# Inner weights of product 4: their stores placed between GpSimd's loads of product 1's inner weights, their rounding spread

## The reference, cut to what matters

```python
q_emb = relu(cond @ W3 + b3)
v = (n * x + sum_over_tokens(x)) * q_emb           # n = 512 tokens
y = relu(v @ W2 + b2)                              # stage 1: 1024 x 1024 weight
base = y @ W_base + b_base                         # stage 2: 1024 x 1024 weight
shared = (y @ A_s) @ B_s
gates = top 2 of softmax(y @ W_router + b_router)
routed = sum over 6 experts of (gate * (y @ A_r[e])) @ B_r[e]
out = x + base + shared + routed
```

## Time and profile before

| what | value |
|---|---|
| median of 3 runs | 1413.12 us (1412.42 to 1414.57) |
| the profiled execution, its own time | 1414.27 us |
| its span, first to last instruction | 1412.4 us |
| mean granted TensorE clock over the span | 0.992 of full speed |
| TensorE busy | 1388.9 us, 98% of the span |
| VectorE, ScalarE, GpSimd busy | 1037.6, 664.0, 79.5 us |
| moved by DMA | 255.63 MB, mean 181 GB/s |

### The profile page before, as it was taken

The page is one execution under the profiler, slowest core; times in us unless marked ns, Lnnn a source line. Parts: engine busy times, 40 slices in busy tenths (PEclk is TensorE's granted clock), DMA queues, the critical chain, the costliest instruction groups (busy, mean ns, idle before and its releaser), DMA issues. The chain is left out here.

```text
span 1412.4 us, 18365 instructions
## 1 busy us (share of the span) xinstructions
PE 1388.9 (98%) x6069; PEld 1139.6 (81%) x6069; DVE 1037.6 (73%) x1700; ACT 664.0 (47%) x1209; POOL 79.5 (6%) x170
## 2 busy tenths in 40 slices
PE   9999999999999999999999998699999999999999
PEld 6888888888888888888888886488888888888887
DVE  6976777675776768678879575777777877778665
ACT  7774756556465664746544232333333432244221
POOL 3000100000000000000000001100000000000000
PEclk9999999999999999999999999799999999999999
DMA  8244836445273542528728379638566485756734
GB/s 314 84 156 119 258 123 179 154 126 156 67 204 117 156 140 76 171 96 274 255 73 262 120 235 320 209 107 266 196 233 239 143 274 183 267 181 188 242 119 160
DMA packets 151327, 255.63 MB, mean 181 GB/s; under 512 B 40416, under 2 KB 40672, under 8 KB 151232
## 3 DMA queue, kind: packets, MB, share of 16 engines
q1 hardware_dynamic: 135680, 199.75, 43.5%
q0 software_dynamic: 14688, 53.48, 12.1%
q10 hardware_dynamic: 864, 1.22, 0.2%
HBM read 171.69 MB, written 82.71 MB: 180 GB/s over the span
## 5 line engine op out<-in xcount | busy, mean ns | idle before, releaser
L2760 PE MATMUL ps<-act_hi,w_hi 128*128 128x512 f32 x1504 | 586.5, 390 | 8.5 <-DVE act_lo L1749 8.5
L2761 PE MATMUL ps<-act_lo,w_hi 128*128 128x512 f32 x1504 | 585.6, 389 | 0.0
L2762 PE MATMUL ps<-act_hi,w_lo 128*128 128x512 f32 x1504 | 585.6, 389 | 0.0
L2760 PEld LDWEIGHTS ps<-act_hi,w_hi 128*128 128x128 f32 x1504 | 282.7, 188 | 69.4 <-DVE act_lo L1749 10.1
L2762 PEld LDWEIGHTS ps<-act_hi,w_lo 128*128 128x128 f32 x1504 | 282.7, 188 | 58.7
L2761 PEld LDWEIGHTS ps<-act_lo,w_hi 128*128 128x128 f32 x1504 | 282.8, 188 | 58.5
L1010 ACT ACTIVATE act_hi<-src 128x512 fp32r<-128x512 f32 x208 | 125.0, 622 | 92.2 <-PE ps L2762 91.6
L1749 DVE TENSOR_TENSOR act_lo<-src,act_hi 128x512 fp32r<-128x512 f32 x192 | 129.5, 685 | 21.2 <-ACT act_hi L1010 21.1
L1029 ACT ACTIVATE yhi<-buf 128x512 fp32r<-128x512 f32 x128 | 80.2, 626 | 81.8 <-PE ps L2762 81.4
L1817 DVE SCALAR_TENSOR_TENSOR buf<-ps,bb_sb,buf 128x512 f32<-128x512 f32 x91 | 67.4, 748 | 64.7 <-PE ps L2762 61.0
L2760 PE MATMUL ps<-act_hi,inner_w 128*128 128x512 f32 x252 | 100.4, 398 | 10.7 <-issue 8.7
(11 more groups left out here) (181 smaller groups left out, 1656.6 us busy)
## 6 DMA issues: line engine op xcount, KB each, us to landing
src<-in_xT SPq DMA_DIRECT2D x224, 256.0 KB, 3.6
y_scratch<-buf SPq DMA_DIRECT2D x128, 256.0 KB, 3.0
src<-y_scratch SPq DMA_DIRECT2D x128, 256.0 KB, 5.2
inner_w<-inner_scratch POOLq DMA_DIRECT2D x63, 512.0 KB, 3.8
outT<-buf SPq DMA_DIRECT2D x115, 256.0 KB, 4.5
inner_scratch<-staged POOLq DMA_DIRECT2D x21, 512.0 KB, 4.9
wl_raw<-in_wbase SPq DMA_DIRECT2D x7, 1024.0 KB, 5.7
partner<-y_scratch POOLq DMA_DIRECT2D x12, 512.0 KB, 5.9
```

Of the source, the lines that this page charges most:

```text
L2760: nc.tensor.matmul(out, wh, a_h, start=start, stop=False, skip_group_check=onto)
L2761: nc.tensor.matmul(out, wh, a_l, start=False, stop=False, skip_group_check=onto)
L2762: return nc.tensor.matmul(out, wl, a_h, start=False, stop=stop, skip_group_check=onto)
```

## The change

Blocks 14 and 15 are rounded behind all four `high(9, 6, j)` and no longer wait for a store; blocks 16 and 17 behind all four `high(10, 0, j)`; block 18 moves from the end of pair 9 into `even`, and 19 and 20 move back by one place each, 20 into the middle of the four roundings of product 2. GpSimd stores 14 and 15 right behind `begin`, 16 and 17 behind `partner`, and 18, 19 and 20 each behind one load of `stream`. `partner4` is loaded between m = 5 and m = 6, in all three of the runs that have one. The two halves of the last store count on one semaphore.

```diff
+        FIRST_OF_TWO = tuple((e_of, 1) for e_of, n_of in RUNS if n_of == 4)
...
-            sp.wait_ge(last_half_stored, 16)
             for j in range(H):
                 sp.wait_ge(buf1_stored[j], 16 * 2 * ALL)
-                sp.wait_ge(buf2_stored[j], 16 * ALL)
+                sp.wait_ge(buf2_stored[j], 16 * (ALL + (j == H - 1)))
...
             def stream(r):
                 for m in range(2, L2):
                     inner_weights(r, m)
+                    if r == EARLY and m < 5:
+                        store_weights(2 * L2 + 2 + m)
+                    if m == 5 and RUNS[r] in FIRST_OF_TWO:
+                        load_partner4(RUNS[r][0])
...
             for e in range(EARLY, len(QUADS)):
                 begin(RUN[e, 1])
+                if e == EARLY:
+                    store_weights(2 * L2)
+                    store_weights(2 * L2 + 1)
                 load_partner(e)
                 if e == EARLY:
-                    for c in range(2 * L2, 3 * L2):
-                        store_weights(c)
-                load_partner4(e)
+                    store_weights(2 * L2 + 2)
+                    store_weights(2 * L2 + 3)
                 stream(RUN[e, 1])
...
                 if k >= 3:
                     act.wait_ge(inner_w_sum, sums_no(c // L2, k - 2))
-                if c >= 2:
+                if c >= 2 and k >= 2 or c // L2 == 1:
                     act.wait_ge(inner_w_stored[c % 2], 16 * (c // 2))
...
                 inner_high(r, 1)
                 if e == EARLY:
-                    inner_weight_high(3 * L2 - 2)
+                    inner_weight_high(2 * L2 + 4)
                 copy_p0(g, 0)
                 lr_high_a(p)
                 inner_high(r, 2)
+                if e == EARLY:
+                    inner_weight_high(2 * L2 + 5)
                 copy_p0(g, 1)
                 copy_p0(g, 2)
-                if e == EARLY:
-                    inner_weight_high(3 * L2 - 1)
                 for j in range(H):
                     high(g, 2, j)
+                    if e == EARLY and j == 2:
+                        inner_weight_high(2 * L2 + 6)
...
                     if g == SECOND - 1 and j in (0, 1):
                         inner_weight_high(L2 + 5 + j)
-                    elif g == SECOND - 1:
-                        inner_weight_high(2 * L2 + j - 2)
+                if g == SECOND - 1:
+                    inner_weight_high(2 * L2)
+                    inner_weight_high(2 * L2 + 1)
                 for j in range(H):
                     high(g + 1, 0, j)
-                    if g == SECOND - 1 and j > 0:
-                        inner_weight_high(2 * L2 + 1 + j)
+                if g == SECOND - 1:
+                    inner_weight_high(2 * L2 + 2)
+                    inner_weight_high(2 * L2 + 3)
...
                 inner_t2(r)
                 if e == EARLY:
-                    inner_weight_low(3 * L2 - 2)
+                    inner_weight_low(2 * L2 + 4)
                 lr_low_a(p)
                 add_p0(r, 0)
                 inner_low(r, 2)
                 inner_t3(r)
+                if e == EARLY:
+                    inner_weight_low(2 * L2 + 5)
                 add_p0(r, 1)
                 for j in range(H):
                     t2(g, j)
-                if e == EARLY:
-                    inner_weight_low(3 * L2 - 1)
                 for j in range(H):
                     low(g, 2, j)
+                    if e == EARLY and j == 2:
+                        inner_weight_low(2 * L2 + 6)
...
                     if g == SECOND - 1 and j == 1:
                         inner_weight_low(2 * L2 + 2)
                         inner_weight_sums(2)
-                    elif g == SECOND - 1 and j > 1:
-                        inner_weight_low(2 * L2 + 1 + j)
+                    elif g == SECOND - 1 and j == 2:
+                        inner_weight_low(2 * L2 + 3)
```

More of the change, by code:

```diff
@@ L272, in adaln_ffn @@
         x21_added = sem("x21_added")
-        last_half_stored = sem("last_half_stored")
         inner_hi_done = sem("inner_hi_done")
@@ L1685, in _ @@
             act.wait_ge(c21_done, four(ALL - 1, H - 1) + 1)
-            act.dma_start(outT[2 * LAST, K - 1, :, T // 2:T], buf2[:, H - 1, T // 2:T]).then_inc(last_half_stored, 16)
+            act.dma_start(outT[2 * LAST, K - 1, :, T // 2:T], buf2[:, H - 1, T // 2:T]).then_inc(buf2_stored[H - 1], 16)
         @block.vector
```

## The result

The changed kernel takes 1397.33 us (median of 4 runs, 1396.03 to 1397.85) against 1413.84 us (4 runs) for the kernel before, measured beside it: ratio 0.9883, interval 0.9865 to 0.9900, that is 16.5 us or 1.2% less. The forecast was 1395.2 us in a range of 1391 to 1402. The profiled execution took 1397.85 us, its span is 1396.0 us, 16.4 us shorter than before, at a mean granted clock of 0.996.

The account below looks back on a forecast made before the run. TensorE, busy 98% of the span, was taken as the bound, so only its stops and slow clock could be won: 4.4 + 2.2 + 8.8 + 2.5 = 17.9 us less, from the median 1413.12 to 1395.2 us, range 1391 to 1402.

Parts of the forecast that it names:

- the clock: TensorE's stop before `low(10, 0, 2)`, shortened to 4.2 us, keeps full clock; inner product 0 takes 2.72 us: 2.2 us less.
- Rival B: The clock falls in what is left of the first stop; the 2.2 us are not won: 1397.5 us; chance 0.27.
- The place of stores 14 and 15: Ahead of `partner` on GpSimd's queue, store 14 lands at 876.2 after 7.0 us; TensorE restarts at 881.1.
- Block 18: Moved from ahead of `inner_low(r, 0)` on VectorE, it lets the first inner product follow the restart 0.6 us sooner.
- The removed wait: Blocks 14 and 15 without waiting for a store: TensorE's 0.46 us wait at 864.45 goes, adding nothing to the sum.
- the place of `partner4`: Loaded between m = 5 and m = 6 in three runs; no margin for m = 6's load, but costed at nothing.
- The second stop: TensorE's wait before inner product 2 in pair 10 goes: 8.8 us, plus 2.5 us for its slow matmuls.
- the first 4.4 us: Passage from pair 9 to 10: the first inner product starts at 886.6 instead of 891.05, 4.4 us earlier.
- Rival E: GpSimd's list becomes a chain, loads m = 3 to 5 late behind stores 18 to 20: slower, 1423 us; chance 0.04.

Follow-up runs that it names:

- The filled kernels: Useless matmuls added to the changed kernel in the gaps before k = 2, k = 3 and inner product 0 (12, 6, 8): 1397.24 us, once more 1396.34 us.
- the repetition: The changed kernel run once more, unaltered, beside the kernel before: 1397.50 us, ratio 0.9896.
- the first of the two later versions: Against the changed kernel, blocks 16 to 20 all rounded in pair 10, `partner` ahead of store 14, stores two, one, two behind loads m = 2 to 4: 1392.26 us.

## Why the prediction was right, and where its sum was not

**The sign, the size and the range** came as forecast, and so did both places in the timeline. Of the sum of 17.9 us, 16.4 came.

**The step that failed** is *the clock*: "I take it that the clock holds, just." That rested on two falls, 4.3 and 4.4 us after the last matmul, taken as a fixed delay, against a stop of 4.2. The delay was not fixed: in the first profile of the changed kernel the fall came 2.5 us after the last matmul, within a stop of 3.7. In the two later profiles of that kernel it came after 4.7 us, with the stop already over. So the comparison failed on both sides: a stop shorter than the delay did not keep the clock, and the three matmuls at its end did not save it. Inner product 0 took 4.47 us, and the term of 2.2 us gave 0.45. Rival B came, with the 1397.5 us that it was given, and its chance of 0.27 was too low. The Trainium skill, "TensorE: Matmul & The Clock Gate", section "Why this matters for your kernels", had spoken for B: idleness between bursts brings the lower clock. By it the sum was about 15.7; the trace agrees, with 16.2 by its terms. The filled kernels show the price in the trace, 1.6 to 2.5 us.

**The place of stores 14 and 15** was right in kind and mis-sized in a term: the landing took 8.7 us (8.3 in the repetition, 869.24 to 877.51) where I took 7.0, between bounds of 2.9 and 9.3. In the first profile it did not show, by luck, since `begin` happened to be 1.7 us early; in the repetition, with `begin` at 868.19, TensorE restarted at 882.37, 1.3 us later than summed. The 4.86 us from ScalarE's start to TensorE's restart held in both. With `partner` ahead of the stores the restart comes about 2 us later.

**Block 18** was right: 0.6 us, 0.8 in the medians. **The removed wait and the place of `partner4`** were right to be priced at nothing; each put back moves nothing that can be measured.

**The second stop** was right to the row: no wait is left there, and with the old order of the queue it is back. What I had not seen is that the two halves are not independent: by the run with the loads behind the stores again, the first 4.4 us count only because the second stop's end no longer hangs on a store.

**Rival E**, GpSimd's list as a chain, did not come; the loads of m = 3 to 5 waited for TensorE alone. It was not far away: the load of m = 6 had 1.52 us to spare, 0.62 in the repetition, and in the first of the two later versions the load of m = 5, behind two stores whose blocks were late, made TensorE wait 2.37 us.

**Not settled:** why `begin` is 1.7 us earlier in some executions than in others, which may be a part of the scatter of 1 to 2 us between runs; and what sets the moment of the fall.

## What to carry to other kernels

On a queue that works in order, read what stands ahead of the late item: loads that are needed soon go ahead of stores that are needed late, and a wait for "all stores" comes behind the last urgent load. Before pricing a stop that is shortened, ask whether the clock outlasts it and the thin work behind it; here a shortened one still cost about 2 us. In the traces these came back with all gaps filled or with the stop removed. Where two stops follow each other, ask what the second one's end hangs on; here a gain at the first was worth nothing until that was changed.

## What the runs showed of the hardware that I had not expected

- The granted clock fell without a long stop too: in the kernel with twelve useless matmuls it fell at 884.6, 1.3 us after a matmul, amid gaps of 1.5 and 2.1 us. From the last matmul before the first stop, where that stop was left unfilled, it fell after 2.5 to 5.0 us.
- It came back at different times: in the changed kernel, with waits of 0.8 and 1.4 us between, 9.0 us after the restart (881.11 to 890.12). Behind the second stop, with dense work, it came back about 5.8 us after the restart in the kernel before (917.06 to 922.8) and 3.0 us after it in the kernel with the loads behind the stores (917.33 to 920.3).
- GpSimd holds back its sixth transfer in this place: after five issued in a row (two of `begin`, three more) the next waits with nothing shown as its releaser, 2.17 us in the earlier trace rows, 3.96 in the changed kernel, whatever the order of stores and `partner`. It went out when the first of the five had landed: that one took 5.0 us from 868.19 in the kernel before (sixth at 873.45) and 6.5 us from 866.48 in the changed kernel (sixth at 873.31). In eight other traces here it went out 0.3 to 0.4 us behind that landing as well.
